# A graph kernel on one core: key/value interleaving moved to ScalarE, a split node sort, and a deeper x pass

## What is computed

```
xn  = layernorm(x)
# graph attention, 4 heads of 64
xp  = xn @ W;  alpha = leaky_relu(a_src[src] + a_dst[dst], 0.2)
w   = exp(alpha - segment_max(alpha, dst));  w /= segment_sum(w, dst)
gnn = elu(segment_sum(xp[src] * w, dst) + bias)
# mixer, 8 heads of 32
q, k, v = split(xn @ w_qkv + b_qkv);  k, v = layernorm(k), layernorm(v)
kv  = k^T v / n;  mix = gelu((q kv + xn) @ w1 + b1) @ w2 + b2 + xn
x   = x + gnn + mix
# feed-forward on the half of the nodes with the largest weight
z = layernorm(x);  weights = z @ wr + br;  idx = top_k(weights, n/2)[:n/2 - 1]
x = x + z + scatter(idx, (gelu(z[idx] @ w1 + b1) @ w2 + b2) * weights[idx])
```

## Time and profile before

| | us |
|---|---|
| median of 3 runs | 3156.56 (3155.16 to 3156.85) |
| the profiled execution | 3154.69 |
| its span | 3152.9 |
| TensorE busy in it | 2120.0 (67%) |
| VectorE | 1898.0 (60%) |
| ScalarE | 732.9 (23%) |
| GpSimd | 2106.3 (67%) |
| chain that ended last | GpSimd 33%, TensorE 23%, VectorE 18%, issue 17%, DMA 5% |

### The profile page before, as it was taken

One profiled execution on the slowest core, in us unless ns is written; L12 is line 12 of the kernel. 1 busy time (PEld: TensorE's weight loads), 2 busy tenths in 40 slices (PEclk: granted clock), 3 DMA queues, 4 the chain that ended last, 5 costly groups with the idle time before them and its releaser, 6 DMA issues.

```text
span 3152.9 us, 38615 instructions
## 1 busy us (share of the span) xinstructions
PE 2120.0 (67%) x8271; PEld 1507.2 (48%) x8271; DVE 1898.0 (60%) x4818; ACT 732.9 (23%) x2199; POOL 2106.3 (67%) x2189
## 2 busy tenths in 40 slices
PE   4457458776767676567766677677764455269998
PEld 3345235544444444445444455455443111168887
DVE  8876558877777777755555555555555688742221
ACT  2134231211111111122221111112210366122222
POOL 4746567777777777777777777777773688043433
PEclk8679679888888888788888888888887678579999
DMA  5447644444444444455555555555543699211111
GB/s 168 143 130 232 115 112 128 125 123 125 125 127 125 125 125 123 133 145 153 153 153 153 153 153 153 155 153 155 151 130 92 172 290 291 77 35 56 55 55 45
DMA packets 259969, 426.67 MB, mean 135 GB/s; under 512 B 73682, under 2 KB 165748, under 8 KB 259764
## 3 DMA queue, kind: packets, MB, share of 16 engines
q0 software_dynamic: 96592, 260.07, 31.4%
q1 hardware_dynamic: 163300, 165.80, 16.6%
HBM read 337.21 MB, written 88.48 MB: 135 GB/s over the span
## 4 chain that ended last, share of the span: by engine, by line
POOL 33%; PE 23%; DVE 18%; issue 17%; DMA 5%; ACT 2%; DVEq 1%; ACTq 1%; POOLq 1%; SPq 0%
POOL G L1234 30%; PE bank L2032 8%; PE bank L916 5%; PE bank L925 5%; DMA G<-tab_d,sidx 3%; POOL G L1211 3%; PE bank L1983 2%; DVE G L1644 2%; PE bank L2013 1%; DVE G L557 1%; DVE G L553 1%; DVE G L554 1%; DVE acc L1660 1%; DVE shared L1562 1%; DVE G L538 1%
## 5 line engine op out<-in xcount | busy, mean ns | idle before, releaser
L1234 POOL DMA_INDIRECT G<-tab_d,sidx x1632 | 1547.0, 948 | 528.4 <-issue 481.8
L2032 PE MATMUL bank<-G,ident 128*128 128x264 f32 x3264 | 921.6, 437 | 598.6 <-DVE G L1644 516.5
L2032 PEld LDWEIGHTS bank<-G,ident 128*128 128x128 f32 x3264 | 657.5, 213 | 860.0 <-issue 511.5
L1644 DVE TENSOR_TENSOR G<-G,bank 128x1024 f32<-128x1024 f32 x408 | 491.2, 1214 | 1.8
L1660 DVE TENSOR_TENSOR acc<-acc,bank 128x264 f32 x816 | 347.9, 426 | 193.6 <-PE bank L2032 163.3
L1899 ACT ACTIVATE bank<-work 128x196 f32<-128x196 f32 x51 | 17.2, 337 | 1210.5 <-DVE work L1631 1210.5
L2013 PE MATMUL bank<-kvw,shared 128*128 128x512 f32 x392 | 188.9, 627 | 38.4 <-DVE shared L1562 27.6
L1615 DVE CAST work<-penI 128x64 f32 (+1 forms) x51 | 12.2, 240 | 316.6 <-DMA G<-tab_d,sidx 313.4
L1983 PE MATMUL bank<-G,acc 128*128 128x264 f32 x392 | 130.3, 489 | 98.2 <-DVE acc L1374 74.4
L889 POOL DMA_INDIRECT out<-G,acc x49 | 48.9, 997 | 192.1 <-DVEq L1004 182.6
L916 PE MATMUL bank<-G 128*128 128x256 f32 (+1 forms) x800 | 174.9, 377 | 0.0
(11 more groups left out here) (397 smaller groups left out, 3099.3 us busy)
## 6 DMA issues: line engine op xcount, KB each, us to landing
G<-tab_d,sidx POOLq DMA_INDIRECT x1632
acc<-x_in SPq DMA_DIRECT2D x98, 256.0 KB, 4.2
shared<-xnT_d SPq DMA_DIRECT2D x98, 256.0 KB, 3.8
accP_d<-acc SPq DMA_DIRECT2D x100, 132.0 KB
tab_d<-acc SPq DMA_DIRECT2D x49, 260.0 KB, 3.5
xnT_d<-acc SPq DMA_DIRECT2D x49, 256.0 KB, 2.4
mix_d<-acc SPq DMA_DIRECT2D x49, 256.0 KB, 2.8
G<-mix_d SPq DMA_DIRECT2D x49, 256.0 KB, 4.3
```

What stands on the lines that cost most here:

```text
L1234: g.indirect_dma_start(out=G[:, s, t, 0:TR], out_offset=None, in_=tab_d, in_offset=bass.IndirectOffsetOnAxis(ap=sidx[:, s, t:t + 1], axis= ...
L1644: v.tensor_tensor(gm[:, q4], gm[:, q4], W1[:, q4][:, :, :, None].to_broadcast([P, 4, HG, CG]), ALU.mult).then_inc(g_ready, 1)
L2032: last = te.matmul(bank[1 + i % NSB][:, 0:ROW], ident[:, :], G[:, s, i * IT + k, :], start=(k == 0), stop=(k == IT - 1))
```

## The change

Six edits:

1. ScalarE interleaves the pairs (`pr`), each half as it lands. SyncE stores them before it loads the K/V weights. VectorE's constants (`pr_end`, `drow`, `ones`) are set at the very start.
2. The sort moves from q = 15 to q = 14. Of the last group's `list_edges` only the count (`count_edges(13)`) is done ahead of it; the rest (`collect_edges(13)`) follows at q = 16. TensorE's products `next_starts` are split: those of `tileF` at q = 4, those of the counts of the first 12 groups before the last count, and the last 8 columns after it. `item_ends` and `item_blocks` stay at q = 17 and 19.
3. The ranking is split: `positions(0, 14)` comes straight after the bases of the keys, then `place_nodes`, then `positions(14, 98)`. GpSimd stores the first 14 blocks after the first of the two signals.
4. The x pass looks one pair further ahead: `norm(q + 3)`, `std(q + 4)` and `turn(q + 2)` in iteration q, with transposes in banks 3 and 1 in turn. SyncE stores the transposed rows one step later.
5. `NKA` is 1: one K/V pair before the lists, four after. The first 16 lists are two groups of 8, whose addresses ScalarE loads before it waits for the stores; GpSimd may gather the first half of chunk 0 after the first 8 lists.
6. In the list of chosen nodes VectorE does the product that GpSimd did. ScalarE loads the table of the feed-forward layer's gelu ahead of its wait.

The core of the diff:

```diff
-    LIST_AT, SORT_AT, CENTRE_AT = 1, 15, 40
-    FLAT = (0, 16, 32, 48, 64, 80, NB)
+    LIST_AT, SORT_AT, CENTRE_AT = 1, 14, 40
+    FP = 14
+    FLAT = (0, 8, 16, 32, 48, 64, 80, NB)
...
-    NKA = 2
+    NKA = 1
...
         def _(act):
             a = nc.scalar
+            act.wait_ge(ld_s, 16)
+            a.copy(pr[:, :, 1], pr_d).then_inc(pair_ready, 1)
+            act.wait_ge(pair_in, 16)
+            a.copy(pr[:, :, 0], pr_s).then_inc(pair_ready, 1)
...
+                dve.wait_ge(hot_ready, 2 * g + 1)
+                v.tensor_tensor(vals[:, s, 0], hit_t[:, s], block_b[:, r, None].to_broadcast([P, GP, NT2]), ALU.mult).then_inc(val_ready, 1)
...
+            sp.wait_ge(pair_ready, 2)
+            sp.dma_start(pair_d[0:EP].rearrange("(p t) k -> p t k", p=P), pr).then_inc(pair_out, 16)
+            sp.wait_ge(end_ready, 1)
+            sp.dma_start(pair_d[EP:EP + P], pr_end).then_inc(pair_out, 16)
             sp.dma_start(wraw, w_qkv.rearrange("(c p) n -> p c n", p=P)).then_inc(ld_kv, 16)
             sp.dma_start(braw, b_qkv[None, :].to_broadcast([P, 3 * D])).then_inc(ld_kv, 16)
-            sp.wait_ge(pair_ready, 1)
-            sp.dma_start(pair_d[0:EP].rearrange("(p t) k -> p t k", p=P), pr).then_inc(pair_out, 16)
-            sp.dma_start(pair_d[EP:EP + P], pr_end).then_inc(pair_out, 16)
...
-            pool.wait_ge(pos_ready, 1)
             for k in range(NGB):
+                if k * GB in (0, FP):
+                    pool.wait_ge(pos_ready, 2 if k else 1)
                 pool.wait_ge(row_ready, (GB * (k + 1) + 1) // 2)
...
+            def count_edges(k):
+
                 dve.wait_ge(win_in[k % 3], 16 * GB * (k // 3 + 1))
+                ends = win[:, k % 3, :, :, 1]
+                lk(v.tensor_tensor(early, ends[:, :, 0:SS - 1], of(nval, k)[:, :, None].to_broadcast([P, GB, SS - 1]), ALU.is_lt))
+                lk(v.tensor_reduce(of(cntF, k), early, AX, ALU.add))
...
+            def positions(lo, hi):
+
+                n = hi - lo
+                ranks, mine = (t.rearrange("p (k b) -> p k b", b=NB)[:, :, lo:hi] for t in (csum, oneh))
+                lk(v.tensor_tensor(ranks, ranks, kbase[:, :, None].to_broadcast([P, KB, n]), ALU.add))
+                lk(v.tensor_tensor(ranks, ranks, mine, ALU.mult))
+                lk(v.tensor_reduce(rsF[:, lo:hi], ranks.rearrange("p k b -> p b k"), AX, ALU.add))
+                v.tensor_copy(pos_i[:, lo:hi], rsF[:, lo:hi]).then_inc(pos_ready, 1)
...
-            for k in range(NGB):
+            for k in range(NGB - 1):
                 events.setdefault(LIST_AT + k, []).append((list_edges, k))
-            for at, f in ((0, degrees), (0, keys), (0, count_keys), (0, place_nodes), (0, rank_keys), (0, positions),
-                          (2, item_ends), (4, item_blocks)):
+            events[SORT_AT] = [(count_edges, NGB - 1)]
+            events[SORT_AT + 2] = [(collect_edges, NGB - 1)]
+            for at, f in ((0, degrees), (0, keys), (0, count_keys), (0, key_bases), (0, first_positions), (0, place_nodes),
+                          (0, other_positions), (3, item_ends), (5, item_blocks)):
                 events.setdefault(SORT_AT + at, []).append((f, None))
...
             dve.wait_ge(flat_done, 1)
-            stage(0, 0)
+            v.tensor_copy(sidx[:, 0, 0:CT // 2], sidxF[:, 0:CT // 2]).then_inc(half_ready, 1)
+            dve.wait_ge(flat_done, 2)
+            v.tensor_copy(sidx[:, 0, CT // 2:CT], sidxF[:, CT // 2:CT]).then_inc(sidx_ready, 1)
             v.memset(accf[:, 0:LATE * ROW], 0.0)
-            dve.wait_ge(flat_done, 2)
+            dve.wait_ge(flat_done, 3)
             stage(1, 1)
...
-                if q + 1 < NP:
-                    turn(q + 1, (q + 1) % 2)
+                if q + 2 < NP:
+                    turn(q + 2, q % 2)
```

More of the change, by code:

```diff
@@ L19 @@
 FAR = 1e30
+GELU_TANH = 11
 LOG_EXP = 6
@@ L782, in threshold_dve @@
             v.sem_inc(perm_ready, 1)
-        def perm_pool(pool):
-            g_ = nc.gpsimd
-            for g in range(NB // GP):
-                s, r = g % 2, slice(g * GP, g * GP + GP)
-                pool.wait_ge(hot_ready, 2 * g + 1)
-                if g >= 2:
-                    pool.wait_ge(perm_mm, g - 1)
-                g_.tensor_tensor(vals[:, s, 0], hit_t[:, s], block_b[:, r, None].to_broadcast([P, GP, NT2]), ALU.mult).then_inc(val_ready, 1)
         def perm_act(act):
@@ L1092, in _ @@
             load_xt(0)
-            for q in range(1, NKA + 1):
+            for q in range(1, NKA):
                 sp.wait_ge(kv_mm, 2 * q)
@@ L1101, in _ @@
                 sp.dma_start(stg[:, lo:hi, :], rows_v[:, lo:hi, 0:W]).then_inc(stg_in[g], 16)
-                if g == 1:
+                if g == 2:
                     sp.dma_start(nodeP[:, 0:NB, :], rows_v[:, :, W:RW]).then_inc(node_in, 16)
-            for q in range(NKA + 1, NK0 + 1):
+            for q in range(NKA, NK0 + 1):
                 sp.wait_ge(kv_mm, 2 * q)
@@ L1226, in gather @@
             def gather(c, s, wait_free):
-                pool.wait_ge(sidx_ready, c + 1)
+                if isinstance(c, int) and c == 0:
+                    pool.wait_ge(half_ready, 1)
+                else:
+                    pool.wait_ge(sidx_ready, c + 1)
                 pool.sem_inc(pace, 1)
                 for t in range(CT):
+                    if isinstance(c, int) and c == 0 and t == CT // 2:
+                        pool.wait_ge(sidx_ready, 1)
                     if wait_free and t % 4 == 0:
@@ L1274, in _ @@
             lk = Chain(dve, vch)
+            v.memset(pr_end, 1 << 20)
+            v.memset(drow[0:1, 0:D], 0.0)
+            v.memset(drow[0:1, D:TR], -FAR).then_inc(end_ready, 1)
+            v.memset(ones[:, :], 1.0)
+            v.memset(onesb, 1.0)
             dve.wait_ge(iota_done, 2)
@@ L1805, in turned @@
                     act.wait_ge(xt_out[q % 4], 16 * (q // 4))
[L1806 removed]
+                a.copy(xt[:, q % 4, :, :], bank[3 - 2 * (q % 2)][:, :].rearrange("p (k n) -> p k n", k=2)).then_inc(xt_ready, 1)
             def node_rows(q):
@@ L1858, in spread_lists @@
                 act.sem_inc(flat_done, 1)
-            spread_lists(0)
-            spread_lists(1)
+            starts = [list_starts(g) for g in (0, 1)]
+            act.wait_ge(row_out, 16 * NB)
+            act.sem_inc(pace, 1)
+            for g in (0, 1):
+                spread_lists(g, starts[g])
+            spread_lists(2, list_starts(2))
             def node_terms(c, s):
@@ L1868, in node_terms @@
                 last.then_inc(nv_ready, 1)
-            for g in range(2, len(FLAT) - 1):
-                if g < NK0:
-                    square(g, slot(g))
-                    root(g, rs[:, slot(g)])
-                spread_lists(g)
-                if g == 3:
+            for g in range(3, len(FLAT) - 1):
+                square(g - 2, slot(g - 2))
+                root(g - 2, rs[:, slot(g - 2)])
+                spread_lists(g, list_starts(g))
+                if g == 4:
                     act.wait_ge(node_in, 16)
@@ L1939, in _, with next_of, next_tiles, next_counts @@
             last.then_inc(ix_pe, 1)
+            def next_of(at, vals, lo, hi):
+                te.matmul(bank[0][:, at + lo:at + hi], shift, vals[:, lo:hi], start=True, stop=False)
+                return te.matmul(bank[0][:, at + lo:at + hi], wrap, vals[:, lo + 1:hi + 1], start=False, stop=True)
+            def next_tiles():
+                pe.wait_ge(rows_done, 1)
+                next_of(0, tileF, 0, NB)
+            def next_counts():
+                pe.wait_ge(rows_done, NGB - 1)
+                next_of(P, cntF, 0, NB - GB - 1)
             def next_starts():
                 pe.wait_ge(ix_dve, 2)
-                for at, vals in ((0, tileF), (P, cntF)):
-                    te.matmul(bank[0][:, at:at + NB], shift, vals[:, 0:NB], start=True, stop=False)
-                    last = te.matmul(bank[0][:, at:at + NB], wrap, vals[:, 1:NB + 1], start=False, stop=True)
-                last.then_inc(ix_pe, 1)
+                next_of(P, cntF, NB - GB - 1, NB).then_inc(ix_pe, 1)
             def bin_starts():
@@ L1966, in blocks_of_items @@
                 for a in (0, 1):
-                    last = te.matmul(bank[1 + a][:, 0:H], ones[:, :], itemc[:, a * H:a * H + H], start=True, stop=True)
+                    last = te.matmul(bank[2 * a][:, 0:H], ones[:, :], itemc[:, a * H:a * H + H], start=True, stop=True)
                 last.then_inc(ix_pe, 1)
@@ L1984, in project @@
                     last.then_inc(xp_ready, 1)
-            steps = {SORT_AT: (next_starts, bin_starts, block_starts), SORT_AT + 2: (blocks_of_items,)}
+            steps = {LIST_AT + 3: (next_tiles,), SORT_AT: (next_counts, next_starts, bin_starts, block_starts), SORT_AT + 3: (blocks_of_items,)}
             turn(0, 0)
+            turn(1, 1)
             for q in range(NP):
```

91 lines of the change are left out of this document (42 added, 49 removed).

## The result

| | us |
|---|---|
| before, median of 4 runs | 3156.51 (3155.16 to 3156.85) |
| changed, median of 4 runs | 3118.44 (3116.78 to 3120.54) |
| ratio | 0.9881, 95% interval 0.9863 to 0.9898 |
| span of the profiled execution | 3115.4 (before 3152.9) |

The sign was right, the size was not. First the timeline from the pairs to the first row store.

What follows compares the result with a forecast made beforehand. GpSimd's gather loop was taken as the bound, so its lasting start must move earlier. X pass 16.9, handover 6.8 and chosen nodes 2.0 sum to 25.7 us: 3154.7 to 3129.0, plus 1.9 gives 3130.9 us; range 3122 to 3143.

Steps and rivals of the forecast that it cites:

- Pairs and sort: Before the x pass: first window gather at 24.1, keys at 157.0, first row store at 170.3 instead of 193.27.
- X pass: Looking two pairs ahead, 2.85 us a pair, nearest the DMA-full 2.83; pass ends at 296.8 against 313.66, gaining 16.9 us.
- the head start: In the x pass: VectorE reaches pair 20 at 208 against 213.25, 5.3 us earlier.
- Handover: From last table row to gather loop: list copies 9.6 us sooner, 2.8 lost to a K/V pair, net 6.8 us.
- The x pass, not the stores, is the next bound: After earlier row stores: 98 stores could be done at 295, but each group of seven needs its 3.5 pairs.
- Half-chunk release at 0: Before the lasting gather start at 437.26: releasing gathers by half a chunk only lengthens GpSimd's stand, worth nothing.
- Chosen nodes: List before the feed-forward stage: product on VectorE alone ends 1 to 2.5 us earlier; 2.0 us taken.
- the second: X pass: engines set 2.5 us a pair, pass ends at 286.6, gain 35.9 us, time 3120.7; chance 0.13.
- Rivals 1: X pass does not quicken, 3.25 us a pair stays; gain 14.1 us, time 3142.5; chance 0.17.
- 3: Handover gives nothing, through late lists or a new 4.62 us gap; gain 18.9 us, time 3137.7; chance 0.10.
- 4: Slower: early stores beside the x pass stretch a pair, at 4.0 us giving 3164.2 us; chance 0.03.
- 5: Gather loop takes the shift back, a later chunk bound by TensorE; only 2 us stay, 3154.6 us; chance 0.02.

Runs made afterwards that it cites:

- p_double: The changed kernel with every block pair's transposed rows stored a second time, to a table nothing reads; 3126.62 us, ratio 0.9914 to the kernel before.
- a_rank_2: The changed kernel with one ranking instead of two (`FP` is 98); 3118.53 us, ratio 0.9883 to the kernel before.
- a_hand_2: The changed kernel with the handover undone (`NKA` 2, first lists one group of 16, addresses after the wait, no half-chunk release); 3124.08 us, ratio 0.9901 to the kernel before.

## Why the prediction was wrong

- **Pairs and sort: right**, to 0.2 us at five places.
- **X pass: the failed step.** "From pair 20 on, 29 pairs" and "I take 2.85": one period for all of them. Iteration 20 began at 206.98 instead of 208.0 (1.0 us). The DMA engines do fill, and the period in which they are full is 2.74, close to the 2.83 that 0.87 x 3.25 gave: the choice of the later limit was right there, and p_double shows it. But it binds for 18 of the 29 pairs. Outside them a pair took 2.48 us. The first three (iterations 20 to 22) took 2.24 each, with no wait for x. The last load of x goes out at 263.93, before the centring of weights ends; after these 6 us of VectorE alone it waits for no x again, and from 275 to 285 TensorE is busy throughout. Charging 2.85 to every pair cost 6.1 us; with the start 7.1 of the 11.8 us between the sum (25.7) and the spans (37.5).
- **Its split: wrong too.** The sum gave 5.3 us to the head start and 11.6 to the depth. With the depth undone the head start is worth 4.0, and the depth 20.0: without it a pair takes the 3.22 us that it took before.
- **Handover: the edit right** (6.8; undone 5.6 in time, 6.6 at the lasting start), the stage not: 9.4. Most of the missing 2.6 us is a K/V product that ran at a higher granted clock (6.39 us at 0.57 before, 5.10 at 0.72) and a load that landed sooner. The products follow the granted clock in all nine traces on the faster chips; what decides the clock there is open, and two kernels with a quick x pass did not get the higher one. The sum had no term for it: this part of the gain is luck.
- **"The x pass, not the stores, is the next bound": half right.** Both are level now (a_rank_2): two stores a pair at 1.28 us are 2.57 us, next to 2.64 for a pair. The row that gave 2.45 us for the engines had this too, GpSimd busy 30.55 us with 32 stores, and the prediction left GpSimd out of that sentence. The split ranking, counted as 8.9 us of an earlier start, buys no time.
- **Half-chunk release at 0:** GpSimd's stand before the lasting start grew from 7.83 to 13.42 us while the start moved by other work, which fits (8.52 in a_hand_2, whose first gather came 11.4 us later and lasting start 6.6), but the run for it is not decisive.
- **Chosen nodes: right**, 2.4 against 2.0 with a range to 2.5. The compare takes 0.87 us in all seven groups, where beside GpSimd it took 2.00 in five of the seven and GpSimd's product 3.05. The Trainium skill ("SBUF — State Buffer", section Who interferes with whom) has a VectorE operation with two inputs in SBUF and a GpSimd operation that reads SBUF exclude each other; both traces agree. **Table load: right**, 0.2.
- **Rivals.** The nearest was the second, at 3120.7, to which 0.13 was given. Its mechanism, that the engines set 2.5 us, fits the eleven pairs outside the stretch (2.48) and not the 18 in it, as p_double shows; that its number is near is partly luck, as its x pass gains 3.1 us too much and its handover 2.6 too little. But its evidence, that a busy share is no measure of the bytes still to be had, held in part: the engines moved 348 GB/s at 1.04 where the prediction reckoned 306. Rivals 1, 3, 4 and 5 are out on the faster chips: a period of 2.64, a handover that gives, no stretch above 3.7 us, and a loop that kept all of the shift.
